# Edge pass of a two-layer graph network: the scale and offset rows of a whole group in four PSUM banks, one projection buffer, the residual add on GpSimd

## The reference, cut to what matters

```python
h = jnp.maximum(_layernorm(x, axis=-1), 0.0)
x = x + _L0_gnn_ref(h, node_type_3, edge_index, edge_type_4, ...)
h = jnp.maximum(_layernorm(x, axis=-1), 0.0)
x = x + _L1_gnn_ref(h, L1_gnn_W1, L1_gnn_b1, L1_gnn_W2, L1_gnn_b2, src, dst)
```

```python
h = jax.nn.gelu(aggr, approximate=False)
trans = (einsum('no,top->tnp', h, Wa) + ba)[node_type, rng]
a = jax.nn.sigmoid(skip)[node_type][:, None]
res = trans * a + node_inp * (1.0 - a)
normed = (res - mu) * jax.lax.rsqrt(var + 1e-05)
return normed * ln_g[node_type] + ln_b[node_type]
```

## Time and profile before

| | us |
|---|---|
| three runs | 3119.45, 3127.17, 3129.85 (median 3127.17) |
| the profiled execution, its own time | 3122.26 |
| its span in the trace | 3120.6 |
| mean granted TensorE clock | 0.769 of full speed |
| PE, DVE, ACT, POOL busy | 61%, 66%, 37%, 59% of the span |
| the edge pass, from the first `wB` matmul to the last `hs` activation | 1762.8 to 2251.9, so 489 |

### The profile page before, as it was taken

How to read it: one execution, slowest core, us unless ns; L and a number is a source line. 1 busy time by engine, 2 the same in 40 slices (tenths; PEclk the granted TensorE clock), 3 DMA queues, 4 the chain that set the end, 5 groups by cost and what they waited for, 6 DMA issues and landing times. The chain is left out here.

```text
span 3120.6 us, 48869 instructions
## 1 busy us (share of the span) xinstructions
PE 1916.5 (61%) x12706; PEld 1487.4 (48%) x12706; DVE 2069.9 (66%) x6764; ACT 1160.4 (37%) x3211; POOL 1837.1 (59%) x2417
## 2 busy tenths in 40 slices
PE   4620006889888889898886378778555553333333
PEld 1100005788888888888886245444334432222222
DVE  7975546888888788788786777777634443333333
ACT  0000005666666666666663245545412221111111
POOL 0003327777777777777774245454466657666766
PEclk9965557999999999999998689898755555555555
DMA  1016755666666666666663244444334442222221
GB/s 48 0 37 232 246 184 146 155 157 155 156 157 155 157 152 157 158 156 151 157 157 93 52 128 116 127 122 121 98 101 116 115 101 65 64 67 63 64 64 49
DMA packets 400270, 374.38 MB, mean 120 GB/s; under 512 B 60254, under 2 KB 342269, under 8 KB 397032
## 3 DMA queue, kind: packets, MB, share of 16 engines
q1 hardware_dynamic: 360856, 276.76, 33.2%
q0 software_dynamic: 31360, 64.76, 10.0%
q10 hardware_dynamic: 7806, 29.98, 2.4%
HBM read 227.43 MB, written 147.13 MB: 120 GB/s over the span
## 5 line engine op out<-in xcount | busy, mean ns | idle before, releaser
L814 POOL DMA_INDIRECT att_xsd<-xt,ends_i x392 | 405.0, 1033 | 179.7 <-issue 136.6
L1669 DVE TENSOR_TENSOR_SCAN conv_sT<-keep,conv_sT,conv_pT 128x128 f32<-128x128 bf16 x390 | 186.5, 478 | 485.3 <-DMA t<-conv_res 193.7
L1650 PE MATMUL conv_pm<-w,conv_sT 128*128 128x128 f32 x784 | 280.1, 460 | 358.6 <-DVE conv_res L1676 226.9
L1650 PEld LDWEIGHTS conv_pm<-w,conv_sT 128*128 128x128 f32 x784 | 196.9, 311 | 450.0 <-issue 321.2
L1008 PE MATMUL att_kvc<-att_hm,w_kv 128*128 128x128 f32 x2352 | 296.3, 276 | 0.0
L1118 DVE TENSOR_TENSOR att_kvm<-att_kvc,att_rel_in 128x1024 f32<-128x1024 f32 x196 | 239.0, 1219 | 62.5 <-PE att_kvc L1021 50.3
L1008 PEld LDWEIGHTS att_kvc<-att_hm,w_kv 128*128 128x128 f32 x2352 | 280.3, 193 | 0.0
L1354 POOL TENSOR_TENSOR edge_glm<-edge_gl,edge_mask 128x1536 f32<-128x1536 f32 (+1 forms) x56 | 153.2, 2736 | 211.9 <-PE edge_pc L1445 205.1
L952 ACT ACTIVATE att_nhb<-att_nxr 128x128 f32<-128x128 f32 x391 | 168.7, 478 | 277.3 <-DMA att_nxr<-xt 276.9
L1107 DVE TENSOR_TENSOR att_hm<-att_hT,att_mask_in_t 128x768 f32<-128x768 f32 x196 | 186.3, 951 | 114.9 <-issue 106.3
L1598 POOL DMA_INDIRECT out_dram<-conv_res,out_i x196 | 198.1, 1011 | 108.6 <-issue 101.3
(11 more groups left out here) (242 smaller groups left out, 5012.0 us busy)
## 6 DMA issues: line engine op xcount, KB each, us to landing
att_mask_in_t<-type_row SPq DMA_DIRECT2D x196, 192.0 KB
xt<-xr ACTq DMA_DIRECT2D x23, 1224.0 KB
att_nxr<-xt SPq DMA_DIRECT2D x97, 262.0 KB
att_rel_in<-rel_row SPq DMA_DIRECT2D x196, 128.0 KB
out_dram<-att_not SPq DMA_DIRECT2D x97, 256.0 KB
ta<-att_nhs SPq DMA_DIRECT2D x97, 256.0 KB
xr<-in_x_dram SPq DMA_DIRECT2D x22, 1088.0 KB
xd_rows<-att_xsd SPq DMA_DIRECT2D x196, 65.5 KB
```

What stands on the lines that cost most here:

```text
L814: pool.indirect_dma_start(out=xsd[:, v, k, :], out_offset=None, in_=xt, in_offset=bass.IndirectOffsetOnAxis(ap=ends_i[:, n, k:k + 1], axis ...
L1650: nc.tensor.matmul(pm[:, k % 2, 0:D], sT[:, k % R], w[:], start=True, stop=True).then_inc(m_ready, 1)
L1669: dve.tensor_tensor_scan(sT[:, n % R], keep[:, n * P:(n + 1) * P], pT[:, n % 2, 0:P], before, ALU.mult, ALU.add).then_inc(s_ready, 1)
```

## The change

- `pg` grows from two banks to four and holds all seven tiles: `gains` runs once a step, behind the first `wB` and `dB` of the step, and DVE multiplies and adds 896 columns at once (before: 512 and 384).
- The banks come from `pc`, now one buffer. The first half of a projection waits until ACT has read the first four tiles of the group before (`y_half`), the second half until it has read all (`y_done`).
- The residual add moves from DVE to POOL, 896 columns in one instruction, in POOL's queue behind both `masked` and ahead of both powers.
- The second statistics of a group run one step later, ahead of the multiply and add of the next group; POOL's second power, `nm2`, `hs` and its store are one step later too, and there are 32 steps in place of 31.
- ACT makes `hb` before `hs`; the factor in `sc3` comes from `ats` in place of `xr`; the semaphores that free `xr` and `oh` change with it, and SP stores `x1` in step g+3 and `hs` in step g+4.

```diff
@@
-            pc = [lp(f"pc{b}", [P, 8, D], F32) for b in two]
-            pg = lp("pg", [P, 4, GW], F32)
+            pc = lp("pc", [P, 8, D], F32)
+            pg = lp("pg", [P, 8, GW], F32)
...
-            steps = range(groups + 3)
+            steps = range(groups + 4)
@@ sync: load(g), and the stores
-                            sp.wait_ge(nm2, g - 3)
+                            sp.wait_ge(x1_done, g - 3)
...
-                            sp.wait_ge(pg_ready, (g - 2) * 2)
+                            sp.wait_ge(pg_ready, g - 2)
@@ gpsimd, after masked(s, 0) and masked(s, 1)
-                        if on(s - 2):
-                            b = (s - 2) % 2
-                            pool.wait_ge(var2, s - 1)
-                            if s >= 4:
-                                pool.wait_ge(nm2, s - 3)
-                            pool.tensor_tensor(rstd[1][b][:], ve[1][b][:], mh[:], ALU.pow).then_inc(rstd2, 1)
...
+                        g = s - 2
+                        if on(g):
+                            pool.wait_ge(pg_read, g + 1)
+                            pool.tensor_tensor(x1[g % 3][:], x1[g % 3][:], xr[g % 4][:, :, 0:D], ALU.add).then_inc(x1_done, 1)
+                        g = s - 3
+                        if on(g):
+                            pool.wait_ge(var2, g + 1)
+                            if g >= 2:
+                                pool.wait_ge(nm2, g - 1)
+                            pool.tensor_tensor(rstd[1][g % 2][:], ve[1][g % 2][:], mh[:], ALU.pow).then_inc(rstd2, 1)
@@ tensor
                     def project(g, ck):
                         j0, j1 = CK[ck]
-                        if ck == 0:
-                            pe.wait_ge(oh_in[g % 3], g // 3 * 48 + 48)
-                            if g >= 2:
-                                pe.wait_ge(y_done, g - 1)
-                                pe.wait_ge(st_done, (g - 1) * 2 - 1)
+                        if g >= 1:
+                            pe.wait_ge(y_done if ck else y_half, g)
                         pe.wait_ge(hb_done, g * G + j1)
...
-                    def gains(g, ck):
-                        j0, j1 = CK[ck]
-                        if g * 2 + ck >= 1:
-                            pe.wait_ge(pg_read, g * 2 + ck)
-                        for j in range(j0, j1):
-                            m = nc.tensor.matmul(pg[:, j - j0], oh[g % 3][:, j * P:(j + 1) * P], tab9[:, CW:CW + GW], start=True, stop=True)
+                    def gains(g):
+                        if g >= 1:
+                            pe.wait_ge(pg_read, g)
+                        for j in range(G):
+                            m = nc.tensor.matmul(pg[:, j], oh[g % 3][:, j * P:(j + 1) * P], tab9[:, CW:CW + GW], start=True, stop=True)
                         m.then_inc(pg_ready, 1)
@@ vector
-                                dve.tensor_tensor(x1[g % 3][:, js], x1[g % 3][:, js], pg[:, 0:w, 0:D], ALU.mult).then_inc(x1_step, 1)
...
-                                m = dve.tensor_tensor(x1[g % 3][:, js], x1[g % 3][:, js], xr[g % 4][:, js, 0:D], ALU.add)
...
+                        g = s - 3
+                        if on(g):
+                            dve.wait_ge(x1_done, g + 1)
+                            combine(1, g, moments(1, g, x1[g % 3]), var2)
                         g = s - 2
                         if on(g):
...
+                            dve.wait_ge(y_done, g + 1)
+                            dve.wait_ge(pg_ready, g + 1)
+                            dve.tensor_tensor(x1[g % 3][:], x1[g % 3][:], pg[:, 0:G, 0:D], ALU.mult).then_inc(x1_step, 1)
+                            dve.wait_ge(x1_step, g + 1)
+                            dve.tensor_tensor(x1[g % 3][:], x1[g % 3][:], pg[:, 0:G, D:GW], ALU.add).then_inc(pg_read, 1)
                         g = s - 1
                         if on(g):
...
+                            combine(0, g, moments(0, g, pc), var1)
```

More of the change, by code:

```diff
@@ L1360, in _ @@
                             masked(s, 1)
[L1361 to L1372 removed]
+                        g = s - 2
[8 more added lines that the diff above has]
+                            pool.tensor_tensor(rstd[1][g % 2][:], ve[1][g % 2][:], mh[:], ALU.pow).then_inc(rstd2, 1)
+                        g = s - 1
+                        if on(g):
+                            pool.wait_ge(var1, g + 1)
+                            if g >= 2:
+                                pool.wait_ge(y_done, g - 1)
+                            pool.tensor_tensor(rstd[0][g % 2][:], ve[0][g % 2][:], mh[:], ALU.pow).then_inc(rstd1, 1)
                 @block.scalar
@@ L1392, in _ @@
                             for j in range(G):
-                                m = nc.scalar.activation(x1[g % 3][:, j], pc[g % 2][:, j], ACT.Identity, bias=nmr[0][g % 2][:, j:j + 1],
+                                m = nc.scalar.activation(x1[g % 3][:, j], pc[:, j], ACT.Identity, bias=nmr[0][g % 2][:, j:j + 1],
                                                          scale=rstd[0][g % 2][:, j:j + 1])
@@ L1399, in _ @@
                             gelu(s, 1)
-                        g = s - 3
+                            act.wait_ge(xr_in[s % 4], s // 4 * 16 + 16)
+                            if s >= 2:
+                                act.wait_ge(pc_ready, (s - 1) * 2)
+                            for j in range(G):
+                                nc.scalar.activation(hb[s % 2][:, j], xr[s % 4][:, j, 0:D], ACT.Relu, bias=xr[s % 4][:, j, C_NA:C_NA + 1],
+                                                     scale=xr[s % 4][:, j, C_RA:C_RA + 1]).then_inc(hb_done, 1)
+                        g = s - 4
                         if on(g):
@@ L1408, in _ @@
                             m.then_inc(hs_done, 1)
-                        if on(s):
-                            act.wait_ge(xr_in[s % 4], s // 4 * 16 + 16)
-                            if s >= 2:
-                                act.wait_ge(pc_ready, (s - 1) * 2)
-                            for j in range(G):
-                                nc.scalar.activation(hb[s % 2][:, j], xr[s % 4][:, j, 0:D], ACT.Relu, bias=xr[s % 4][:, j, C_NA:C_NA + 1],
-                                                     scale=xr[s % 4][:, j, C_RA:C_RA + 1]).then_inc(hb_done, 1)
                 @block.tensor
@@ L1444, in project @@
                             for t in range(TYPES):
-                                m = nc.tensor.matmul(pc[g % 2][:, j], glm[ck][:, j - j0, t], w_a[:, t],
+                                m = nc.tensor.matmul(pc[:, j], glm[ck][:, j - j0, t], w_a[:, t],
                                                      start=False, stop=j == j1 - 1 and t == TYPES - 1)
                         m.then_inc(pc_ready, 1)
-                    def gains(g, ck):
-                        j0, j1 = CK[ck]
-                        if g * 2 + ck >= 1:
-                            pe.wait_ge(pg_read, g * 2 + ck)
-                        for j in range(j0, j1):
-                            m = nc.tensor.matmul(pg[:, j - j0], oh[g % 3][:, j * P:(j + 1) * P], tab9[:, CW:CW + GW], start=True, stop=True)
+                    def gains(g):
+                        if g >= 1:
+                            pe.wait_ge(pg_read, g)
+                        for j in range(G):
+                            m = nc.tensor.matmul(pg[:, j], oh[g % 3][:, j * P:(j + 1) * P], tab9[:, CW:CW + GW], start=True, stop=True)
                         m.then_inc(pg_ready, 1)
@@ L1461, in _ @@
                         if on(s - 2):
-                            gains(s - 2, 0)
+                            gains(s - 2)
                         if on(s):
                             spread(s, 1)
-                        if on(s - 1):
-                            project(s - 1, 0)
-                        if on(s - 2):
-                            gains(s - 2, 1)
-                        if on(s - 1):
-                            project(s - 1, 1)
+                        g = s - 1
+                        if on(g):
+                            pe.wait_ge(oh_in[g % 3], g // 3 * 48 + 48)
+                            project(g, 0)
+                            project(g, 1)
                 @block.vector
@@ L1490, in gathered, with moments @@
                                                ALU.mult, ALU.add).then_inc(scan_done, 1)
-                    def spreads(k, g, of, done, then):
+                    def moments(k, g, of):
                         for j in range(G):
@@ L1497, in spreads, with combine @@
                         m.then_inc(st_done, 1)
-                        dve.wait_ge(st_done, done)
+                        stats[0] += 1
+                        return stats[0]
+                    def combine(k, g, at, then):
+                        dve.wait_ge(st_done, at)
                         for j in range(G):
```

39 lines of the change are left out of this document (10 added, 29 removed).

## The result

| | before | changed |
|---|---|---|
| median of four runs, us | 3125.47 | 3178.39 (3175.48 to 3185.18) |
| ratio | | 1.0174, 95% interval 1.0161 to 1.0186 |
| span of the profiled execution, us | 3120.6 | 3176.1 |
| edge pass, first multiply to last `hs`, us | 487.0 | 547.5 |
| 24 steps of it, us each | 17.07 | 19.03 |

The account below looks back on a forecast made before the run. Bound: a loop of waits in each edge-pass step, no engine full. New loop 16.8 us plus clock 1.8 makes 18.6 against 17.07; 25 steps give +38, drain +8, so +46 on 3122.3: 3168, given as 3170; range 3125 to 3198.

Parts of the forecast that it names:

- The ring through POOL: Edge pass: projection, POOL's product, add and powers, DVE's shift, ACT's four tiles, next projection; 16.8 us at full clock.
- DVE's work: Edge pass: DVE's own work in a step falls from 13.3 us to about 10.5.
- rival D: POOL's new add holds DVE's L1506, delaying DVE by 2 us, but no time alters; no chance given.
- some 15 us: Edge pass: the step that DVE's lighter work alone would give, without the loop over POOL's queue.
- The gap ahead of the projection: Edge pass: PE idles 3.8 us between the second dB and the next projection.
- The clock: Edge pass: PE's idling lowers the clock over the next projection, making the 16.8 us step 18.6 us.
- I take 1.8, near the measured end: Low-clock cost per edge-pass step: 1.8 us, between at least 1.6 and at most 3.4 to 4.2.
- rival C: Clock stays low through most of the projection: step 20.2 to 20.5 us, 3205 to 3220 us; chance 0.13.
- 25 steps were counted: Edge pass: 25 steps, third to last that loads a group, at 1.5 us more each, +38 us.
- The drain: End of the edge pass: one step more, +2.9 to +12.3 us, taken as +8.
- Rival A: Edge pass: clock stays up or falls only now and then; 0 to +8 us, 3122 to 3135; chance 0.13.
- rival B: POOL's loop is shorter than its rows add up to: 15.0 to 15.5 us, time 3085 to 3115; chance 0.12.

Follow-up runs that it names:

- filled kernel: Changed kernel with 12 matmuls that nobody reads ahead of each first half of a projection; ratio to the kernel before 1.002, step 16.79 us.
- the add on DVE: Changed kernel with the residual add back on DVE as one 896-column instruction, POOL's add taken out; ratio to the kernel before 1.0027, step 17.06 us.
- power-first kernel: Changed kernel with POOL's power for the first statistics directly behind the second product, ahead of the residual add; ratio to the kernel before 1.0035, step 17.08 us.
- version with every gap filled: Changed kernel with POOL's two powers ahead of the add and 2 + 1 + 8 unread matmuls in PE's gaps; ratio to the kernel before 0.981.
- 12 in a gap of 3.16 us: Kernel before with 12 unread matmuls behind the first gains of a step, where PE idles; ratio to the kernel before 0.9876, step 15.47 us.
- half of the filling: Kernel before with 6 unread matmuls behind the first gains of a step, where PE idles; ratio to the kernel before 0.999, step 17.00 us.
- single buffer alone: Kernel before with only one projection buffer and its waits for ACT's reads; pg, adds and queue order as before; ratio to the kernel before 1.0211.
- both powers first: Changed kernel with POOL's two powers ahead of the add and 8 unread matmuls ahead of the projection; ratio to the kernel before 0.9877.

## Why the prediction was right

- **The ring through POOL.** Forecast 16.8 us at full clock, found 16.5. The add took 1.945 us on average (taken: 2.0), the powers 1.49 and 1.48. The estimate of 2.055 us from the Trainium skill, "GPSIMD Engine Reference", section "Performance versus the Vector engine", used as its fixed part 156 ns that the page gives for VectorE, not for GpSimd; in plain proportion its 4497 ns would make 4497 x 896/2048 = 1967 ns, an estimate too, and the trace has 1945. The gaps between POOL's instructions, set at 0.15, are not there: each starts 0.02 to 0.05 us before the end shown for the one ahead. From the power to the projection it was 1.83 (taken: 1.78). The steps of 16.58 us in the filled kernel, and the 14.6 at full clock with the add on DVE, bear the ring out.
- **DVE's work** fell as said: two instructions of 1.09 us (taken: 1.1), and DVE waits for `rstd1` instead. The hold of L1506, rival D, is real (1.19 us) and costs nothing in the changed kernel, since DVE waits afterwards anyway. In the power-first kernel the hold of the shift makes ACT idle 0.96 us ahead of its read of `pc`; no run takes away that hold alone. The "some 15 us" for DVE's loop without POOL had no sum behind it. The version with every gap filled does all of DVE's work in steps of 14.41, so DVE's loop is at most that; it decides nothing in the changed kernel.
- **The gap ahead of the projection**: 3.25 to 3.74 us, 3.5 on average, forecast 3.8.
- **The clock** is the term that was too small. The step "I take 1.8, near the measured end" measured 2.6 on average, between 1.8 and 3.4 from step to step; that lies inside the prediction's own bounds of 1.6 and 4.2. Its reason, that the clock had been back before half of the products in the step of before, leaned on a step in which the low stretch began with the second `dB` ahead of the projection. Now it covers the projection from its first matmul on, and in the longest steps most of its first half. One step of five reaches the 3.4 us at which rival C begins, two more have 2.8 and 2.9. The filled gap showed this part directly: -2.24 us a step with every wait left in place.
- **Number of steps and the drain.** 25 steps were counted, 24 lie between like points. The drain grew by 12.5 and not by 8, a whole drain step, the upper end that had been worked out. The end of the pass shows the parts:

```profile
2281.83 1.95 POOL L1364 TENSOR_TENSOR edge_x<-edge_x,edge_xr 128x896 f32<-128x896 f32 x1 [5.10 <-DVE edge_x L1539]
...
2300.37 0.17 DVE L1523 TENSOR_TENSOR edge_sc<-edge_rstd,ats 128x7 f32<-128x7 f32 x1 [3.51 <-POOL edge_rstd L1370]
...
2306.64 2.80 ACT L1416 ACTIVATE edge_hs<-edge_x,edge_nmr,edge_sc 128x128 f32<-128x128 f32 x7 [3.06 <-DMA ta<-edge_hs]
```

Ahead of the last `hs` ACT idles 3.06 us. Its shift is ready at 2304.88, so 1.8 us of that are the wait for the store of the `hs` before, since there is one `hs` buffer; no term of the prediction had that. In the variants with the changed order of steps the drain is nearly as long, 50 to 55 us; none of them was made to shorten it.

The terms together: 46.9 + 12.5 + 1.2 = 60.6 in the pass, of which 55.5 reach the span, where 46 had been forecast. In a step the clock was set 0.8 us too low and the ring 0.3 too high; the drain was 4.5 too low. That makes the forecast nearly 15 us too low for the pass, and 5 us outside it (the earlier start and the rest, which no term had) take a third of that back. So the mechanism and the order of the costs were forecast, while part of the nearness of 46 and 53 is luck: errors of opposite sign.

- **Rival A** (0 to +8) fell with the clock, **rival B** (the ring shorter than its rows) fell with the 2.90 us for which DVE waits for the power and with steps above 18 us.

## What to carry to other kernels

When a buffer is given up, follow the ring that its new wait closes through every queue it passes, and put nothing in those queues ahead of the instruction that the ring waits for: here a 2 us add and the power of the second statistics, both ahead of the power that the ring needs, cost more than all the work saved on DVE. A wait ahead of matmuls on the critical ring was paid twice here, once as idle time and once in the clock behind it. When a loop at full clock is compared with a measured one, the clock's share has to be taken out of both. Where the wait can't be removed, matmuls into an unused corner of PSUM can pay for themselves: 12 in a gap of 3.16 us did, 6 did not.

## What was not expected of the hardware

- **Four kernels, one step.** The kernel before, the one with half of the filling, the power ahead of the add and the add on DVE all settle at 17.06 to 17.08 us a step, with full-clock loops of 15.45, 15.45, about 15.0 and 14.6. For the last two that is the step less the extra time of the three parts of the projection's first half, 2.05 and 2.45 us. The clock falls once a step in all four, and the step doesn't follow the work; in the two kernels with a clock of 1.00 it does: 15.47, 14.41. A loop shorter by up to 0.8 us measured as nothing here. It is no general limit: the changed kernel (16.5 at full clock) and the single buffer alone (16.8) take 19.03 and 19.36. Why it is this length was not tried.
- **The cycle of five steps** (18.32, 19.35, 19.89, 18.54, 19.46) came back on a second chip to 0.01 us. The single buffer alone has a cycle of three steps instead (18.57, 19.49, 19.96).
- **Half of the filler did nothing.** 12 matmuls in the gap gave a clock of 1.00 and -39 us, 6 gave 0.90 and nothing. The Trainium skill, "TensorE: Matmul & The Clock Gate", section "HAM oscillation — how this bites in real kernels", describes a kernel whose waits for DMA bring the clock down at every tile, and advises restructuring the loop so that the engine stays busy. The rows here agree that a wait in each step brings the clock down in each step, and show besides that useless matmuls can serve as well.
- **A held instruction of seven columns.** DVE's shift took 1.67 us beside POOL's add and 0.17 alone; with both powers first the factor took 1.92.
